# Retention layer plus gated feed-forward on one core: the slot reordered from tile 11 on, y of tiles 9 to 28 turned through DRAM, all x1 turned on TensorE, new drain

## What is computed

```python
q1, k1 = apply_rotary(x @ Wq, x @ Wk); v = x @ Wv            # per head, chunks of 64
attn    = (q @ k.T) * D                                       # D: causal, decaying
o       = attn @ v + (q * cross_q) @ S                        # S: state, 64 x 128 a head
S       = gC * S + (k * cross_k).T @ v
y       = rmsnorm(o, gn_weight) * silu(x @ Wg)                # 512 wide
x1      = layernorm(x + y @ Wo)
h       = silu(x1 @ wg.T) * (x1 @ wu.T)                       # int weights, scaled by 1/127
out     = layernorm(x1 + h @ wd.T)
```

## Time and profile before

| | |
|---|---|
| median of 3 runs | 418.9 us (418.05 to 420.15) |
| profiled execution | 419.4 us, of which 417.7 us from the first to the last instruction (the span) |
| TensorE matmul busy | 407.2 us (98%), 4634 matmuls |
| TensorE weight loads busy | 388.4 us (93%) |
| VectorE busy | 328.9 us (79%) |
| ScalarE busy | 259.9 us (62%) |
| GpSimd busy | 183.4 us (44%) |
| granted TensorE clock | 0.998 of full |
| chain that ended last | TensorE 86%, DMA 4%, VectorE 3%, the rest 2% or less each |

### The profile page before, as it was taken

One profiled execution on the slowest core, in us unless ns is written; L12 is line 12 of the kernel. 1 busy time (PEld: TensorE's weight loads), 2 busy tenths in 40 slices (PEclk: granted clock), 3 DMA queues, 4 the chain that ended last, 5 costly groups with the idle time before them and its releaser, 6 DMA issues.

```text
span 417.7 us, 12797 instructions
## 1 busy us (share of the span) xinstructions
PE 407.2 (98%) x4634; PEld 388.4 (93%) x4634; DVE 328.9 (79%) x944; ACT 259.9 (62%) x790; POOL 183.4 (44%) x330
## 2 busy tenths in 40 slices
PE   8999999998999999999999999999999999999994
PEld 6899999998999999999999999999999999999893
DVE  4989676767877887788887788888878878875974
ACT  6678645477666665666666666666657665754551
POOL 2432244355244553444455344445534444443563
PEclk9999999999999999999999999999999999999999
DMA  7941010010221413123141312313222231310001
GB/s 277 346 160 53 0 52 2 29 39 14 52 78 34 98 49 89 41 52 103 35 96 45 87 49 49 106 35 95 52 57 73 48 82 32 72 35 9 13 26 54
DMA packets 53776, 28.39 MB, mean 68 GB/s; under 512 B 36816, under 2 KB 49232, under 8 KB 53712
## 3 DMA queue, kind: packets, MB, share of 16 engines
q1 hardware_dynamic: 53568, 27.48, 23.5%
q10 hardware_dynamic: 144, 0.07, 0.1%
HBM read 19.14 MB, written 8.39 MB: 66 GB/s over the span
## 4 chain that ended last, share of the span: by engine, by line
PE 86%; DMA 4%; DVE 3%; SPq 2%; issue 2%; ACT 1%; POOL 1%; POOLq 0%; DVEq 0%; ACTq 0%
PE b_rows L595 28%; PE b_ffn L595 19%; PE b_rows L613 18%; PE b_turn L832 3%; PE b_head L865 3%; PE b_head L873 2%; PE b_state L892 2%; DMA k_rows<-wf_int 2%; PE b_head L790 1%; PE b_rows L609 1%; PE b_head L886 1%; DMA wf_int<-in_w_proj 1%; PE b_ffn L779 1%; SPq L528 1%; PE b_turn L626 1%
## 5 line engine op out<-in xcount | busy, mean ns | idle before, releaser
L2136 POOL TENSOR_TENSOR h_lo<-wf_int,h_hi 128x256 fp32r<-128x256 f32 x96 | 70.7, 749 | 111.2 <-ACT h_hi L1289 111.2
L595 PE MATMUL b_ffn<-x1T_hi,wf_hi 128*128 128x256 f32 x384 | 92.4, 280 | 0.1
L595 PE MATMUL b_ffn<-x1T_lo,wf_hi 128*128 128x256 f32 x384 | 91.8, 278 | 0.0
L1278 ACT ACTIVATE wf_int<-b_ffn 128x256 f32<-128x256 f32 x96 | 36.9, 384 | 67.2 <-PE b_ffn L595 67.1
L595 PEld LDWEIGHTS b_ffn<-x1T_hi,wf_hi 128*128 128x128 f32 x384 | 72.3, 188 | 0.6 <-DVE x1T_lo L1767 0.2
L595 PEld LDWEIGHTS b_ffn<-x1T_lo,wf_hi 128*128 128x128 f32 x384 | 72.3, 188 | 0.0
L613 PE MATMUL b_rows<-wp_hi,xT_hi 128*128 128x256 f32 x230 | 66.4, 289 | 1.2 <-issue 1.2
L613 PE MATMUL b_rows<-wp_hi,xT_lo 128*128 128x256 f32 x244 | 66.5, 277 | 0.0
L613 PE MATMUL b_rows<-wp_lo,xT_hi 128*128 128x256 f32 x230 | 63.8, 277 | 0.0
L1698 DVE TENSOR_TENSOR wf_int<-b_ffn,wf_int 128x256 f32<-128x256 f32 x96 | 40.2, 418 | 23.8 <-ACT wf_int L1278 23.2
L613 PEld LDWEIGHTS b_rows<-wp_hi,xT_hi 128*128 128x128 f32 x230 | 43.1, 188 | 5.7 <-issue 5.2
(11 more groups left out here) (196 smaller groups left out, 1156.8 us busy)
## 6 DMA issues: line engine op xcount, KB each, us to landing
xT_raw<-in_xT SPq DMA_DIRECT2D x16, 256.0 KB, 3.0
x_sb<-in_x SPq DMA_DIRECT2D x16, 256.0 KB, 3.2
out<-wf_int SPq DMA_DIRECT2D x30, 128.0 KB, 2.9
k_rows<-wf_int SPq DMA_DIRECT2D x22, 128.0 KB, 1.7
qkT<-k_rows SPq DMA_DIRECT2D x88, 32.0 KB, 2.2
wf_int<-in_w_ffn SPq DMA_DIRECT2D x6, 384.0 KB, 6.4
wf_int<-in_w_proj SPq DMA_DIRECT2D x6, 256.0 KB, 4.3
x_rows<-wf_int SPq DMA_DIRECT2D x10, 128.0 KB, 1.7
```

What stands on the lines that cost most here:

```text
L595: mm = pe.matmul(dst, a, b, start=(i == 0 and j == 0 and not begun), stop=(i == n - 1 and j == len(passes) - 1 and not more), skip_group_c ...
L1278: act.activation(act_g[:, u], b_ffn[u][:, 0:256], ACT.Silu, scale=SCALE).then_inc(silu_done[j], 1)
L2136: pool.tensor_tensor(h_lo[:, ring, hb], h_full[:, u], h_hi[:, ring, hb].bitcast(F32), ALU.subtract).then_inc(h_split[j], 1)
```

## The change

From slot 11 on (TURNED) a new list, `turned_slot`, replaces `packed_slot` on all engines; slots 9 and 10 keep the old one. TensorE's slot s is now: keys and queries of tile s, `turn_x1` of tile s-4, `heads`, gate/up 0, gate/up 1, values, gate/up 2, down projection of tile s-7, output projection of tile s-3, gate of tile s. y of tiles 9 to 28 (`moved_y`, 20 tiles) is turned as the keys are: `block_y` on VectorE (a 128x512 block transpose), `write_y` and the four DMAs of `move_y` on the SP queue, each with 16x32 runs of 128 bytes where those of the keys have 8x32. `split_y` for these tiles reads SBUF in two halves (odd heads stand with their two 64-row halves swapped) on ScalarE and on VectorE. x1 of all tiles is turned on TensorE again, one slot later than before, and `write_x1`, `move_x1` and `block_x1` go. The order of `b_rows` banks within the slot follows the new order. In `heads` the second state update goes to `b_turn`. GpSimd's slot begins with `inv_std_1` of tile s-4 and `inv_std_2` of tile s-8 and splits xT one tile further ahead. The drain, which is the list after slot 31, is written anew on every engine: same steps, other order, and it begins with `turn_y` of tile 29 and has one more `turn_x1` (tile 28).

```diff
+TURNED = PACKED + 2
...
-        x1_blocks = wf_int[:, 5 * 512 + 256:6 * 512].bitcast(F32)
-        x1T_raw = wf_int[:, 6 * 512:6 * 512 + 256].bitcast(F32).rearrange("p (k n) -> p k n", k=KD)
+        y_blocks = wf_int[:, 7 * 512:8 * 512].bitcast(F32)
+        yT_raw = wf_int[:, 8 * 512:9 * 512].bitcast(F32)
...
+        def by_parity(ap):
+            return ap.rearrange("p (c a b n) -> p a c b n", c=H // 2, a=2, b=2)
...
+            if a == 1 and n >= TURNED - 1:
+                return b_turn[:, 0:256]
...
-        def moved_x1(n):
-            return n % 2 == 0 and CHUNKED <= n < NT - 5
-        def x1_moves(n):
-            return 16 * (P // BLOCK) * ((n - CHUNKED) // 2 + 1)
-        def x1_turns(n):
-            return sum(not moved_x1(i) for i in range(n))
         def packed_rows(s, k):
-            return b_rows[(5 * s + k) % 2]
+            place = (2, 0, 3, 1, 4)[k] if s >= TURNED else k
+            return b_rows[(5 * s + place) % 2]
+        def moved_y(n):
+            return TURNED - 2 <= n < NT - 3
+        def y_moves(n):
+            return 16 * (P // BLOCK) * (n - TURNED + 3)
+        def y_turns(n):
+            return sum(not moved_y(i) for i in range(n))
...
-            def write_x1(n):
-                sp.wait_ge(x1_blocked, (n - CHUNKED) // 2 + 1)
-                sp.dma_start(x1_rows, x1_blocks).then_inc(x1_written, 16)
-            def move_x1(n):
-                sp.wait_ge(x1T_split, n - 1)
-                sp.wait_ge(x1_written, 16 * ((n - CHUNKED) // 2 + 1))
-                blocks = x1_rows.rearrange("(i r) (k j c) -> r k i j c", i=P // BLOCK, k=KD, c=BLOCK)
+            def write_y(n):
+                sp.wait_ge(y_blocked, n - TURNED + 3)
+                sp.dma_start(y_rows, y_blocks).then_inc(y_written, 16)
+            def move_y(n):
+                sp.wait_ge(yT_split, n)
+                sp.wait_ge(y_written, 16 * (n - TURNED + 3))
+                blocks = y_rows.rearrange("(i r) (h j c) -> r h i j c", i=P // BLOCK, h=H, c=BLOCK)
                 for j in range(P // BLOCK):
-                    dst = x1T_raw[j * BLOCK:(j + 1) * BLOCK].rearrange("p k (i c) -> p k i c", c=BLOCK)
-                    sp.dma_start(dst, blocks[:, :, :, j]).then_inc(x1_moved, 16)
+                    dst = yT_raw[j * BLOCK:(j + 1) * BLOCK].rearrange("p (h i c) -> p h i c", h=H, c=BLOCK)
+                    sp.dma_start(dst, blocks[:, :, :, j]).then_inc(y_moved, 16)
...
-                turn_here = s >= PACKED and moved_x1(s - 3)
-                if turn_here:
-                    write_x1(s - 3)
                 if moved(s):
                     write_k(s)
                     move_k(s)
-                if turn_here:
-                    move_x1(s - 3)
+                if s >= TURNED and moved_y(s - 2):
+                    write_y(s - 2)
+                    move_y(s - 2)
...
             def turn_x1(s, q, t):
...
-                if exists(n) and not moved_x1(n):
+                if exists(n):
...
             def heads_ready(s):
...
-                if s < NT:
+                if s < TURNED:
                     pe.wait_ge(h_ready[1], s - FFN_LAG)
+                elif s < NT:
+                    pe.wait_ge(yT_split, min(s - 3, TURNED - 2))
+                    pe.wait_ge(next_kept, nexts_to(n - 1))
...
             def gate_up_block(s, q, t, j, wide, last_waits=None):
...
-                    behind = 3 if moved_x1(s - 3) else behind
...
+            def turned_slot(s, wide):
+                q, t = s // TS, s % TS
+                keys_and_queries(s, q, t)
+                if s > TURNED:
+                    turn_x1(*at(s - 4, X1T_LAG))
+                heads_ready(s)
+                heads(s)
+                gate_up_block(*at(s, -1), 0, wide)
+                gate_up_block(*at(s, -1), 1, wide)
+                if s == TURNED:
+                    turn_y(*at(s - 3, 2))
+                if not moved(s):
+                    turn_qk(s, q, t)
+                project(s, q, t, 1, v_done)
+                gate_up_block(*at(s, -1), 2, wide)
+                if has_q(s, t):
+                    pe.wait_ge(k_parts, s - NATURAL + 1)
+                down(*at(s - 7, DOWN_LAG), wide, free=(rot_parts, s + 1))
+                attention_out(*at(s - 3, 2), free=(v_copied, s + 1))
+                project(s, q, t, 2, g_done)
...
             def split_y(s, q, t):
...
-                    act.wait_ge(yT_done, n + 1)
+                    if moved_y(n):
+                        act.wait_ge(y_moved, y_moves(n))
+                    else:
+                        act.wait_ge(yT_done, y_turns(n) + 1)
                     if exists(n - 1):
                         act.wait_ge(wo_done, n)
+                    if moved_y(n):
+                        src, dst = by_parity(yT_raw), by_parity(yT_hi[:])
+                        act.copy(dst[:, 0], src[:, 0])
+                        act.copy(dst[:, 1], src[:, 1, :, ::-1]).then_inc(yT_high, 1)
+                        return
                     act.copy(yT_hi[:], b_turn[:]).then_inc(yT_high, 1)
...
+            def turned_slot(s):
+                q, t = s // TS, s % TS
+                b, tb = s - 1, (s - 1) % TS
+                gate_v(*at(s, -1))
+                if exists(s + 3):
+                    split_xT(*at(s, 3))
+                if exists(s - 4):
+                    split_x1T(*at(s - 4, X1T_LAG))
+                turn_q(s, q, t, 0)
+                mean_squares(*at(s - 2, 1))
+                gate(b, tb, 0)
+                split_y(*at(s - 3, 2))
+                if not moved(s):
+                    keep_qk(*at(s, 1))
+                turn_q(s, q, t, 1)
+                copy_v(s, q, t)
+                gate(b, tb, 1)
+                split_h(b, tb, 0)
+                gate(b, tb, 2)
+                split_h(b, tb, 1)
+                split_h(b, tb, 2)
...
+                    if moved_y(n):
+                        src, high, low = by_parity(yT_raw), by_parity(yT_hi[:].bitcast(F32)), by_parity(yT_lo[:])
+                        dve.tensor_tensor(low[:, 0], src[:, 0], high[:, 0], ALU.subtract)
+                        dve.tensor_tensor(low[:, 1], src[:, 1, :, ::-1], high[:, 1], ALU.subtract).then_inc(yT_split, 1)
+                        return
                     dve.tensor_tensor(yT_lo[:], b_turn[:], yT_hi[:].bitcast(F32), ALU.subtract).then_inc(yT_split, 1)
...
+            def block_y(n):
+                dve.wait_ge(y_ready, n + 1)
+                if moved_y(n - 1):
+                    dve.wait_ge(y_moved, y_moves(n - 1))
+                dve.transpose(y_blocks, y[:]).then_inc(y_blocked, 1)
...
+            def turned_slot(s):
+                q, t = s // TS, s % TS
+                b, tb = s - 1, (s - 1) % TS
+                if s == TURNED:
+                    split_x1T(*at(s - 4, X1T_LAG))
+                    gated_output(*at(s - 3, 1))
+                else:
+                    norm_1(*at(s - 4, X1T_LAG))
+                norm_2(*at(s - 8, DOWN_LAG + 1))
+                packed_rotate_k(s, q, t)
+                packed_rotate_q(s, q, t)
+                if s > TURNED:
+                    split_x1T(*at(s - 4, X1T_LAG))
+                add_first_half(s - 1)
+                add_second_half(s - 1)
+                sum_k(s, q, t)
+                if moved(s):
+                    block_k(s)
+                mask(*at(s - 1, 1))
+                hidden(b, tb, 0)
+                split_y(*at(s - 3, 2))
+                gated_output(*at(s - 2, 1))
+                if moved_y(s - 2):
+                    block_y(s - 2)
+                hidden(b, tb, 1)
+                residual_2(*at(s - 7, DOWN_LAG))
+                stats_2(*at(s - 7, DOWN_LAG))
+                hidden(b, tb, 2)
+                moments_2(s - 7, (s - 7) % TS)
+                turned_sines(s, q, t)
+                residual_1(*at(s - 3, 2))
+                moments_1(s - 3)
+                add_q(s, q, t)
...
+            def turned_slot(s):
+                b, tb = s - 1, (s - 1) % TS
+                if s > TURNED:
+                    inv_std_1(*at(s - 4, 2))
+                    inv_std_2(*at(s - 8, DOWN_LAG + 1))
+                if exists(s + 3):
+                    split_xT(*at(s, 3))
+                rms_norm(*at(s - 2, 1))
+                split_h(b, tb, 0)
+                split_h(b, tb, 1)
+                split_h(b, tb, 2)
```

The drain on TensorE, its first steps:

```diff
             def drain(wide):
-                down(*at(NT - 7, DOWN_LAG), wide, (0,), free=(g_gated, NT), more=True)
+                turn_y(*at(NT - 3, 2))
+                down(*at(NT - 7, DOWN_LAG), wide, (0,), free=(z1_ready, NT - 3), more=True)
                 down(*at(NT - 7, DOWN_LAG), wide, (2,), begun=True, more=True)
-                gate_up_block(*at(NT - 1, 0), 1, wide)
-                turn_y(*at(NT - 3, 2))
-                gate_up_block(*at(NT - 1, 0), 2, wide)
                 heads_ready(NT)
                 last_recalls()
...
```

(8 more changed lines are left out.)

162 lines of the change are left out of this document (82 added, 80 removed).

## The result

The changed kernel takes 433.38 us (median of 4 runs, 431.85 to 435.06), where the kernel before, run beside it, took 418.78 (418.05 to 420.15): ratio 1.0346, 95% interval 1.0299 to 1.0392. The forecast was 425.0 with a range to 429.0: the direction was right, the size 8.4 us short, and the time lies outside the range. The profiled execution took 433.49 us, its span 431.7, the granted clock 0.994.

What follows compares the result with a forecast made beforehand. TensorE bounded the kernel; afterwards VectorE's, GpSimd's and ScalarE's loops would. Slots 12 to 28 +4.9, 29 to 31 +1.0, drain +0.2 on 419.4 gave 425.5, less 0.5: 425.0 us; own range 421 to 429, 8-in-10 range 411.3 to 429.

Steps and rivals of the forecast that it cites:

- TensorE's part: TensorE: 20 turns of y removed at 0.44 us, 10 of x1 added at 0.23: -6.5 us, slot about 11.95.
- Loops 1 and 2: Slot rounds through x1 on VectorE and GpSimd (12.13 us) and through ScalarE (12.16), both longer than TensorE's 11.95.
- The collision: Slots 12 to 28: VectorE's norm_2 stands behind GpSimd's split of xT, +0.40 us in both loops, slot 12.56.
- SP queue: DMA queue for keys and y: y lands in time, slack 2.5 us; as the bound, 432 us, chance 0.08.
- Free at either end: SP queue: y DMAs at 0.63 or 1.25 us each hold up nothing, just so at the slow end.
- loops without the collision: Rival for the steady slots: the two loops set a 12.16 us slot, 418.2 us in all; chance 0.15.
- Slot 11 is a mixed slot; I take 0: Entry, where the old order meets the new: no cost, bounds -0.5 and +1 us.
- The exit: Slot 31, summed like 29 and 30 (12.16 for 11.83), and the drain: +0.2 for one x1 turn, reordering 0.
- the third loop: Not in the prediction: output projection, residual, norm_1, turn_x1, then TensorE's row to the next output projection; 12.04 us.

Runs made afterwards that it cites:

- v2: f3 with two VectorE steps moved: turned_sines behind moments_1, the keys' rotation ahead of norm_2; 430.4 us, ratio 1.026.
- v1: f4 with two VectorE steps moved: turned_sines behind moments_1, the keys' rotation ahead of norm_2; 425.3 us, ratio 1.014.
- f3: Changed kernel with all y turned on TensorE, GpSimd's xT split behind rms_norm, and heads(11) behind gate/up 0 and 1; 432.4 us, ratio 1.030.
- f4: f1 with y taken later, but earlier than in f2, on ScalarE (behind the queries' second turn) and VectorE; 424.3 us, ratio 1.013.
- exit edit: On the changed kernel, TensorE's turn_qk(31) waits only for y up to tile 9 split, not y of tile 28; alone 432.6 us, ratio 1.032.
- e1: Changed kernel with GpSimd's split of xT moved behind rms_norm in its slot; 431.7 us, ratio 1.029.
- v3: Changed kernel with two VectorE steps moved: turned_sines behind moments_1, the keys' rotation ahead of norm_2; 430.6 us, ratio 1.023.
- e2: Changed kernel with GpSimd doing inv_std_2 of tile s-8 before inv_std_1 of tile s-4; 435.8 us, ratio 1.039.
- f1: e1 plus the exit edit, and heads(11) put behind its slot's gate/up 0 and 1; 430.0 us, ratio 1.024.
- f2: f1 with the turned y taken only behind hidden block 1, on ScalarE and on VectorE; 437.2 us, ratio 1.042.

## Why the prediction was right and where it failed

**TensorE's part, right for y, short for x1.** 0.44 us per turn of y: v2 against v1 shows 12.5 against 12.04 in the quiet slot. (f3 is 8.1 us longer than f4 in all, near the 8.8 of 20 turns, but by chance: f3 lacks the exit edit, and 3.8 us of its longer span lie behind heads(31).) The turn of x1 was priced at 0.23; in its new place, right ahead of the 64x64 stretch, it takes 0.43 from its start to the stretch (220.32, its row above, to 220.75). 0.10 of that the last product paid there before (0.21 from its start to the stretch at 162.27, where 0.11 is usual), so the turn costs 0.33. The 11.95 counted for a slot of TensorE lies between what v1 shows, 11.79 where matmuls start 0.113 apart and 12.14 where they start 0.118 apart.

**Loops 1 and 2, right.** 12.13 and 12.16 forecast without the collision; e1's quiet slots are 12.0 to 12.2 and f4's 12.1. That those of v1 and v3 fall to 12.04 when `turned_sines` and the rotation leave the line shows that it is this line. Which of the two loops is the longer, the runs do not tell.

**The collision, right** in place, order and size: 0.81 beside 0.40, 0.07 between the starts, -0.4 when removed. The row agrees with the Trainium skill (SBUF — State Buffer, section "SBUF: two separate sides"): the second instruction stands until the first has gone, and ends 0.15 behind it. e2's rows agree with it too, with GpSimd as the second. Slots 12 to 28 were to cost +4.9 and cost +5.4 (y late in four of them, and two at 0.118); slots 29 and 30 took 12.2 as forecast.

**SP queue, half right.** "Free at either end" was true for the keys' and y's issue (0.64 us per y DMA, the fast bound) and for the 12.5 us slot, where ScalarE waits for y 1.2 us in 17 slots. It was false as a margin: the row of one transfer was taken as the time of all. The write of the keys lands after 2.3 us in the median where it was 1.7 before, the last read of y after 3.4 in f1, and y is wanted first by an engine behind which others queue. With a 12.1 us slot ScalarE waits 8 to 9 us for it, and slots 12 to 28 are 10 to 12 us longer than 17 quiet ones (e1 less its lower clock, and f1). So the rival "loops without the collision", 418.2, could not have come true by removing the collision: e1 is that case, and its two runs took 428.6 and 434.7. The section of the Trainium skill on which the forecast leaned for the cost of an issue is about DMAs that GpSimd issues, and these are issued by the SP queue; here the 0.64 us decides.

**"Slot 11 is a mixed slot; I take 0" failed:** +3.9, where the bounds were -0.5 and +1. The inputs that the first new slot wants had not been followed: keys of tile 10 that were just sent to DRAM (2.36 us) and GpSimd's xT (0.74 us).

**The exit failed too:** +0.5 was forecast for slot 31 and the drain, +3.9 measured. Slot 31 was summed as slots 29 and 30 are, and the wait of turn_qk for `yT_split` was not read: the change turned it from a wait for a y that TensorE had itself turned in that slot into one on a DMA. It cost 2.8 us and, behind it, 1.7 us of lower clock, where the forecast had no term for the clock. Without it the stretch from heads(31) to the end loses nothing against counted work (52.4 against 47.3 + 5.7). The granted clock is 0.993 or 0.994 in all four runs of the changed kernel and 0.998 in the profiled one of the kernel before, so the fall is probably in each of them, which is not shown: only one was profiled. The two ends together are 7.3 of the 8.4 us by which the forecast fell short.

**Left out:** the third loop. It lies 0.1 us under the two counted and did not set the changed kernel's slot, so it is no part of the miss; it is why the change can't give much even when mended. At best it gains 0.23 a slot (12.27 to 12.04), not the 0.32 counted, and no kernel here beats the one before: the best, f4, is at 1.013.

Open: why single transfers land 1 to 2 us later than the median, why matmuls start 0.113 us apart in some slots and 0.118 in others, and why the clock falls behind one pause and not behind another of the same length.

## What to carry to other kernels

At the seam between two orders, and at the last slot of one, list what the first new instruction of each engine waits for and when it was started; a seam is costed by that, not by the work in it. When a step moves from an engine to a DMA, search every wait on its semaphore, those on a bank's reuse above all, and place the step that takes the result as late in its engine's queue as its readers allow, but not later (f4 against f1, and f2). When a removed stall does not shorten the whole, look for what now comes late, and tell the two apart with the mean and the shortest slot side by side. Read the granted clock of a long stretch too before giving all of its length to a wait.
